# First tile of an attention tower: rows of ten 1000-row tables chosen by one-hot matmuls from whole tables, in place of gathers

## The chip, the core and the metric

The kernel runs on one core of a Trainium2 chip, in Bass, with the order of the work on each engine written out by hand. TensorE (PE) multiplies matrices from SBUF into PSUM, VectorE (DVE) and ScalarE (ACT) do elementwise work, GpSimd (POOL) issues the indirect DMAs here, and SyncE (SP) issues the plain ones. The metric is the device time of one execution in microseconds (us).

## What is computed

Thirty-three embedding tables of width 128 are looked up with 1024 x 33 ids; ten of the tables have 1000 rows, the others 1250, 12500 or 125000. All 528 pairs of the 33 rows of a sample are multiplied, sent through a layer, scored against a feature of the sample, weighted by a softmax and summed; a small network follows.

```
e = stack([tbl_f[ids[:, f]] for f in range(33)], axis=1)       # 1024 x 33 x 128
row, col = triu_indices(33, k=1)                               # 528 pairs
inner = e[:, row] * e[:, col]
fm = relu(einsum('bpd,ad->bpa', inner, attn_W) + attn_b)
attn = softmax(einsum('ba,bpa->bp', gnn_feature, fm), axis=1)
out = einsum('bp,bpd->bd', attn, inner) * 100
h = concatenate([gnn_feature, out, gnn_feature], axis=1)
h = relu(h @ W_top1 + b_top1); h = relu(h @ W_top2 + b_top2)
y = h @ W_top3
```

## The kernel before

The 1024 samples are taken in 8 tiles (t) of 128. A tile has 32 steps of 4 samples, so there are 256 steps (S), and each step works on 4 x 528 = 2112 columns.

**Rows into columns.** For each tile POOL gathers the 33 tables' rows into `x_rows`, one indirect DMA for each field (L259), in five groups of up to 8 fields: group c holds fields 8c to 8c+7, and group 4 the one field 32. When a group has landed (`rows_gathered`), PE transposes each field with the identity `ident` into one of three PSUM buffers `ring` (`transpose_x`, L574), and ACT copies the buffer into `xt` (`evacuate_xt`, L328). Groups 0 and 1 are copied once more behind field 32 (`repeat`, L318). `xt` has two buffers, one for each of two tiles. SP stores `x_rows` as a whole to DRAM (`store_rows`, L213) when all 33 gathers have landed; the gathers of the next tile wait for that store.

**A step.** DVE multiplies pairs of `xt` into `inner` (`product`, L405). Of the 5 chunks of a step (424 or 416 columns) some are multiplied by the attention weights directly in fp32 (L534, "native"; each shows as two records in the trace); for the rest ACT rounds `inner` to `inner_hi` (L298), DVE subtracts for `inner_lo` (L412), and PE makes three fp32r matmuls (L541 to L543). The first step has 4 native chunks, the second 3, later ones 1 or 2. ACT applies the relu into `fm` (L290), and PE reduces two steps at a time against `gnn_blocks` into `scores` (L564). Jobs of other tiles are laid between the steps: the transposes of tile t+1 at steps 18 to 26 of tile t, and `fields` (L592, fp32 matmuls of 128 x 128 with 128 columns) and the small network for tile t-1.

**The beginning.** SP issues the loads: ids, attention weights, features, bias, and then the six loads of the network (`mlp_weights_loaded`, 96 when all have landed), L215 to L224. PE transposes the features (L626). ACT waits for the network's loads before it rounds the attention weights (L349); DVE then makes `attn_wt_lo` (L467), adds two blocks of `w1_sb` (L470) and fills `gnn_blocks` (L419, L422). PE waits for these and for the network's loads before its first transpose of `x_rows`. DVE begins `product(0)` when all five groups are in `xt`, and PE begins `hidden(0)` after it.

## Time and profile before

| | us |
|---|---|
| runs before, median of 3 (lowest to highest) | 1273.31 (1273.05 to 1274.86) |
| the profiled execution, its own time | 1276.58 |
| its span in the profile | 1274.3 |
| first product on DVE starts | 52.18 |
| first matmul of a step on PE starts | 54.64 |

The span is the stretch that the profile covers; 2.3 us of the profiled execution's own time lie around it. An idle time in a row stands behind the instruction that ended it, with what released it. "Share of 16 engines" for a DMA queue is the time that its packets took over the stretch times 16.

### The profile page before, as it was taken

The page shows a single profiled execution, that of the slowest core. Times are in us where ns is not written, and L with a number is a line of the kernel's source. Part 1 is how long each engine was busy: PE and PEld are TensorE (multiplying, and loading weights), DVE is VectorE, ACT ScalarE, POOL GpSimd, SP SyncE. Part 2 cuts the span into 40 slices and gives each one's busy share as a digit, 9 for nine tenths or more (in the row PEclk, how much of TensorE's full clock was granted, in tenths as well). Part 3 has the DMA queues.
Part 4 walks back from the last instruction along what each step waited for, and adds up shares of the span by engine and source line. Part 5 has one row for each costly group of instructions (what it writes and reads, how often), then busy time and mean ns, then how long its engine had stood idle before and what let it go on. Part 6 is the DMA issues. An engine that isn't in the chain of part 4 may idle for free.

```text
span 1274.3 us, 21264 instructions
## 1 busy us (share of the span) xinstructions
PE 1207.8 (95%) x8752; PEld 902.5 (71%) x8752; DVE 1150.6 (90%) x643; ACT 1018.7 (80%) x1038; POOL 465.7 (37%) x271
## 2 busy tenths in 40 slices
PE   1499999999999999999999999999999999999998
PEld 1277777777777777777767777677776777777776
DVE  2399899998999989998999989999899998999974
ACT  1288998778887888878897788877888788887882
POOL 6586684018810387006840088102880000000000
PEclk9999999999999999999999999999999999999999
DMA  4213211311103111131102211031111300012100
GB/s 107 101 34 96 55 30 28 110 36 30 30 18 126 30 27 32 30 106 36 32 21 58 93 30 32 18 110 41 30 32 31 107 17 1 1 30 57 31 1 1
DMA packets 54287, 58.47 MB, mean 46 GB/s; under 512 B 10536, under 2 KB 48560, under 8 KB 53168
## 3 DMA queue, kind: packets, MB, share of 16 engines
q1 hardware_dynamic: 45728, 39.81, 10.5%
q0 software_dynamic: 8448, 17.32, 5.2%
q8 instruction: 69, 1.13, 0.4%
q14 instruction: 26, 0.21, 0.1%
q10 hardware_dynamic: 16, 0.00, 0.0%
HBM read 36.12 MB, written 17.31 MB: 42 GB/s over the span
## 4 chain that ended last, share of the span: by engine, by line
PE 78%; ACT 7%; issue 7%; DVE 6%; POOL 2%; DMA 0%; DVEq 0%; ACTq 0%; POOLq 0%
PE scores L564 18%; PE ring L534 16%; PE ring L541 12%; PE ring L542 11%; PE ring L543 11%; PE ring L592 3%; ACT fm L290 3%; DVE inner L405 3%; POOL x_rows L259 2%; PE ring L574 2%; ACT inner_hi L298 2%; DVE inner_lo L412 2%; PE ring L610 1%; DVE attn L447 1%; PE scores L621 1%
## 5 line engine op out<-in xcount | busy, mean ns | idle before, releaser
L290 ACT ACTIVATE fm<-ring,attn_b_sb 128x848 f32<-128x848 f32 (+1 forms) x640 | 596.9, 971 | 182.1 <-PE ring L534 175.7
L405 DVE TENSOR_TENSOR inner<-xt 128x2112 f32<-128x2112 f32 x256 | 602.7, 2354 | 67.5 <-ACT xt L328 37.4
L259 POOL DMA_INDIRECT x_rows<-in_tbl,ids_all x264 | 463.2, 1754 | 490.9 <-PE ring L574 401.2
L412 DVE TENSOR_TENSOR inner_lo<-inner,inner_hi 128x1688 fp32r<-128x1688 f32 (+4 forms) x256 | 467.0, 1824 | 25.8 <-ACT inner_hi L298 22.8
L541 PE MATMUL ring<-inner_hi,attn_wt_lo 128*128 128x424 f32 (+1 forms) x971 | 434.8, 448 | 4.2 <-ACT fm L290 3.5
L298 ACT CAST inner_hi<-inner 128x1688 fp32r<-128x1688 f32 (+4 forms) x256 | 392.3, 1532 | 5.1 <-DVE inner L405 5.0
L542 PE MATMUL ring<-inner_lo,attn_wt_hi 128*128 128x424 f32 (+1 forms) x971 | 344.3, 355 | 0.0
L543 PE MATMUL ring<-inner_hi,attn_wt_hi 128*128 128x424 f32 (+1 forms) x971 | 344.1, 354 | 0.0
L534 PE MATMUL ring<-inner,attn_wt 128*128 128x424 f32 (+1 forms) x618 | 276.6, 544 | 10.2 <-issue 6.5
L564 PE MATMUL scores<-fm,gnn_blocks 128*32 128x264 f32 x4096 | 254.6, 389 | 5.5 <-ACT exp_pairs L305 5.5
L541 PEld LDWEIGHTS ring<-inner_hi,attn_wt_lo 128*128 128x128 f32 x971 | 182.8, 188 | 71.8 <-issue 39.1
L542 PEld LDWEIGHTS ring<-inner_lo,attn_wt_hi 128*128 128x128 f32 x971 | 183.3, 189 | 43.5 <-issue 40.3
L564 PEld LDWEIGHTS scores<-fm,gnn_blocks 128*32 128x32 f32 x4096 | 119.9, 109 | 107.2 <-issue 13.9
L543 PEld LDWEIGHTS ring<-inner_hi,attn_wt_hi 128*128 128x128 f32 x971 | 182.5, 188 | 5.5
L534 PEld LDWEIGHTS ring<-inner,attn_wt 128*128 128x128 f32 x618 | 104.8, 190 | 85.5 <-issue 76.9
L274 POOL MEMSET inner<- 128x2048 f32 x1 | 1.8, 1811 | 279.0 <-PE ring L543 279.0
L574 PE MATMUL ring<-ident,x_rows 128*128 128x128 f32 x264 | 39.2, 292 | 34.1 <-DMA x_rows<-in_tbl,ids_all 31.3
L328 ACT COPY xt<-ring 128x1024 f32<-128x1024 f32 (+1 forms) x40 | 38.5, 966 | 31.6 <-PE ring L574 20.8
L574 PEld LDWEIGHTS ring<-ident,x_rows 128*128 128x128 f32 x264 | 33.0, 151 | 39.6 <-DMA x_rows<-in_tbl,ids_all 25.2
L592 PE MATMUL ring<-attn_t,x_fields 128*128 128x128 f32 x480 | 58.3, 275 | 1.1 <-issue 1.1
L592 PEld LDWEIGHTS ring<-attn_t,x_fields 128*128 128x128 f32 x480 | 58.0, 191 | 1.7 <-issue 1.5
L447 DVE TENSOR_TENSOR attn<-ring,xt 128x1024 f32<-128x1024 f32 x32 | 39.0, 1219 | 3.2 <-PE ring L592 2.9
(50 smaller groups left out, 250.3 us busy)
## 6 DMA issues: line engine op xcount, KB each, us to landing
x_dram<-x_rows SPq DMA_DIRECT2D x8, 2112.0 KB, 6.6
x_fields<-x_dram SPq DMA_DIRECT2D x120, 128.0 KB, 3.0
x_rows<-in_tbl,ids_all POOLq DMA_INDIRECT x264
attn_t<-attn_turned SPq DMA_DIRECT2D x112, 32.0 KB, 1.9
w_sb<-in_W_top SPq DMA_DIRECT2D x2, 512.0 KB
x_rows<-x_dram SPq DMA_DIRECT2D x8, 128.0 KB, 3.9
x_fields<-in_r_gnn_feature SPq DMA_DIRECT2D x1, 512.0 KB
h<-in_W_top SPq DMA_DIRECT2D x1, 256.0 KB
```

What stands on the lines that cost most here:

```text
L259: nc.gpsimd.indirect_dma_start(out=x_rows[:, f, :], out_offset=None, in_=tables[f], in_offset=bass.IndirectOffsetOnAxis(ap=ids_all[:, t, f ...
L290: nc.scalar.activation(dst, slot(("hidden", pair, j))[:, :, 0:n], ACT.Relu, bias=attn_b_sb[:, 0:1]).then_inc(s_fm, 1)
L298: nc.scalar.copy(inner_hi[:, S % HI_BUFS, 0:COLS - at], inner[:, S % INNER_BUFS, at:]).then_inc(s_hi, 1)
L405: nc.vector.tensor_tensor(dst, a, b, ALU.mult).then_inc(s_inner, 1)
L412: nc.vector.tensor_tensor(inner_lo[:, S % LO_BUFS, 0:COLS - at], inner[:, S % INNER_BUFS, at:], inner_hi[:, S % HI_BUFS, 0:COLS - at].bitc ...
L534: nc.tensor.matmul(dst, attn_wt[:], inner[:, S % INNER_BUFS, begin:end], start=True, stop=True)\
L541: nc.tensor.matmul(dst, attn_wt_lo[:], hi, start=True, stop=False)
L542: nc.tensor.matmul(dst, attn_wt_hi[:], lo, start=False, stop=False)
L543: nc.tensor.matmul(dst, attn_wt_hi[:], hi, start=False, stop=True).then_inc(s_hidden, 1)
L564: last = nc.tensor.matmul(scores[I * j:I * j + I, h, 0:HALF], block_of(s, j), fm[:, S % FM_BUFS, at:at + HALF], start=s == 0, stop=s == ST ...
L574: last = nc.tensor.transpose(to[:, n // 4, n % 4 * P:(n % 4 + 1) * P], x_rows[:, FU * c + n, :], ident[:])
L592: last = nc.tensor.matmul(bank[:, h, to:to + QS * I], x[:, n, :], own[:, :, n, :], start=True, stop=True)
```

## The change

For the first tile alone, the ten tables with 1000 rows (fields 2, 17, 21, 22, 23, 32, 26, 27, 29, 31, in this order) are loaded whole, 512,000 bytes each: 125 partitions with 8 rows of the table (4096 contiguous bytes) on each. The loads are ten DMAs that ACT issues as its first instructions. They land in `fm` and in `inner`, which are not used yet.

DVE puts the ids of the first tile on diagonals (`spread_ids`: memset, two casts and ten multiplications of 128 x 128, ahead of its other work), PE spreads them over all partitions with matmuls against ones (`put_ids_over`), and DVE compares them with row numbers from an `iota` on POOL (`choose`: one instruction of 128 x 1024 for each table, three buffers in the unused half of `xt`). PE then makes 8 accumulating fp32 matmuls for each table, with 125 rows of the table as weights and the one-hot columns moving. The result is the transposed field.

POOL gathers the other 23 fields first and these ten after them (their rows are still needed in `x_rows` for the store to DRAM, which now waits for them too). The groups of the first tile are taken in the order 0, 1, 2, 4, 3. PE gets 30 filler matmuls (ident by ident, 128 columns) before its wait for the last group's gathers and 10 after its transposes. `product(0)` is cut in two, one sample's 528 columns first, and PE's first chunk waits for the first piece alone.

```diff
-    units = [("x_t", 0, c) for c in range(XJ)]
+    units = [("x_t", 0, c) for c in XT_FIRST]
...
+            def gather_rows(t, f, signal):
...
                     for f in range(FU * c, FU * c + fields_in(c)):
-                        nc.gpsimd.indirect_dma_start(
-                            out=x_rows[:, f, :], out_offset=None, in_=tables[f],
-                            in_offset=bass.IndirectOffsetOnAxis(ap=ids_all[:, t, f:f + 1], axis=0),
-                        ).then_inc(s_gather[c], 16)
+                        if t > 0 or f not in ONE_HOT:
+                            gather_rows(t, f, s_gather[c])
+                if t == 0:
+                    for f in ONE_HOT:
+                        gather_rows(0, f, s_late)
...
+            for k, f in enumerate(ONE_HOT):
+                used = tables[f].shape[0] // PARTS
+                act.dma_start(small[k][0:used], tables[f].rearrange("(p c) d -> p c d", c=PARTS)).then_inc(s_tables[k], 16)
             act.wait_ge(s_small, 48)
             act.wait_ge(s_weights, 96)
...
+            def choose(k):
+                dve.wait_ge(s_ids_over, k // 4 + 1)
+                dve.wait_ge(s_row_of, 2)
+                if k >= CHOSEN:
+                    dve.wait_ge(*taken(k - CHOSEN))
...
+                nc.vector.tensor_tensor(chosen[k % CHOSEN], over, rows, ALU.is_equal).then_inc(s_chosen, 1)
...
+            def product_first():
+                x = xt[:, 0, 0:GROUPS, :]
+                dst = inner[:, 0].rearrange("d (g k f) -> d g k f", g=GROUPS, k=K)
+                for own, signal in ((slice(0, 1), s_first), (slice(1, GROUPS), s_inner)):
...
             gnn_block(0)
+            for k in range(len(ONE_HOT)):
+                choose(k)
             dve.wait_ge(s_xt_out, XJ)
             dve.wait_ge(s_repeat, K // FU)
-            product(0)
+            product_first()
             product(1)
...
+            def warm_up(n):
+                for _ in range(n):
+                    nc.tensor.matmul(scores[:, 0, 0:P], ident[:], ident[:], start=True, stop=True)
...
+                if t == 0:
+                    for f in own:
+                        if f in ONE_HOT:
+                            k = ONE_HOT.index(f)
+                            used = tables[f].shape[0] // PARTS
+                            pe.wait_ge(s_tables[k], 16)
+                            pe.wait_ge(s_chosen, k + 1)
+                            for p in range(PARTS):
+                                last = nc.tensor.matmul(home(f), small[k][0:used, p, :], chosen[k % CHOSEN][0:used, p, :],
+                                                        start=p == 0, stop=p == PARTS - 1, skip_group_check=True)
...
+                if t == 0 and c == XT_FIRST[-1]:
+                    warm_up(30)
+                pe.wait_ge(s_gather[c], rows_in(t, c))
...
             pe.wait_ge(s_setup, 6)
             pe.wait_ge(s_weights, 96)
-            for c in range(XJ):
+            for c in XT_FIRST[0:3]:
                 transpose_x(0, c)
-            pe.wait_ge(s_zero, 3)
+            put_ids_over(8, len(ONE_HOT))
+            for c in XT_FIRST[3:]:
+                transpose_x(0, c)
+            warm_up(10)
+            pe.wait_ge(s_zero, 4)
```

On PE, from the end of the setup to the first chunk of step 0, before (L574 are the transposes, L534 the first chunk):

```order
L574 MATMUL ring<-ident,x_rows 128x128 [waits rows_gathered0,mlp_weights_loaded,setup_copied]
L574 MATMUL ring<-ident,x_rows 128x128 x7
L574 MATMUL ring<-ident,x_rows 128x128 [waits rows_gathered1]
L574 MATMUL ring<-ident,x_rows 128x128 x7
L574 MATMUL ring<-ident,x_rows 128x128 [waits rows_gathered2]
L574 MATMUL ring<-ident,x_rows 128x128 x7
L574 MATMUL ring<-ident,x_rows 128x128 [waits x_t_evacuated,rows_gathered3]
L574 MATMUL ring<-ident,x_rows 128x128 x7
L574 MATMUL ring<-ident,x_rows 128x128 [waits x_t_evacuated,rows_gathered4]
L534 MATMUL ring<-inner,attn_wt 128x424 [waits x_t_evacuated,inner_ready,zeros_made]
```

The same place now, its beginning (L702 are the one-hot matmuls, with the table in `fm` as weights and the one-hot columns in `xt`; L711 the transposes; table 0 is field 2, table 1 field 17):

```order
L702 MATMUL ring<-xt,fm 128x128 [waits small_table_loaded0,one_hot_columns_made,mlp_weights_loaded,setup_copied]
L702 MATMUL ring<-xt,fm 128x128 x7
L711 MATMUL ring<-ident,x_rows 128x128 [waits rows_gathered0]
L711 MATMUL ring<-ident,x_rows 128x128 x6
L711 MATMUL ring<-ident,x_rows 128x128 [waits rows_gathered1]
L711 MATMUL ring<-ident,x_rows 128x128 x7
L702 MATMUL ring<-xt,fm 128x128 [waits one_hot_columns_made,small_table_loaded1]
```

and its end, from the last of the ten tables (L675 are the fillers, L638 the first chunk):

```order
L702 MATMUL ring<-xt,inner 128x128 [waits one_hot_columns_made,small_table_loaded9]
L702 MATMUL ring<-xt,inner 128x128 x7
L675 MATMUL scores<-ident 128x128 x30
L711 MATMUL ring<-ident,x_rows 128x128 [waits rows_gathered3]
L711 MATMUL ring<-ident,x_rows 128x128 x3
L675 MATMUL scores<-ident 128x128 x10
L638 MATMUL ring<-inner,attn_wt 128x424 [waits x_t_evacuated,first_products_ready,zeros_made]
```

Ten of the 33 transposes are replaced by 80 matmuls, which stand between the remaining 23, and 40 fillers are added. On ACT, before, the start of the program is the wait for the network's loads:

```order
L349 ACT_TABLE_LOAD [waits setup_copied,mlp_weights_loaded]
L349 CAST attn_wt_hi<-attn_wt 128x128 [waits small_inputs_loaded]
L328 COPY xt<-ring 128x128x8 [waits x_t_filled]
```

Now the ten loads of whole tables stand ahead of it:

```order
L405 DMA fm<-in_tbl 125x1024 x6
L405 DMA inner<-in_tbl 125x1024 x4
L409 ACT_TABLE_LOAD [waits setup_copied,mlp_weights_loaded]
L409 CAST attn_wt_hi<-attn_wt 128x128 [waits small_inputs_loaded]
L385 COPY xt<-ring 128x128x8 [waits x_t_filled]
```

Nothing is waited for ahead of them.

## Rows read from the trace of the kernel before

**Rows 1.** The page: busy time, TensorE by fortieth of the span, chain by engine.

```profile
PE 1207.8 (95%) x8752; PEld 902.5 (71%) x8752; DVE 1150.6 (90%) x643; ACT 1018.7 (80%) x1038; POOL 465.7 (37%) x271
...
PE   1499999999999999999999999999999999999998
...
PE 78%; ACT 7%; issue 7%; DVE 6%; POOL 2%; DMA 0%; DVEq 0%; ACTq 0%; POOLq 0%
```

**Rows 2.** The chain in order of time, 0 to 60 us: start, us, what.

```profile
4.50 1.14 POOL x_rows L259
5.94 0.94 POOL x_rows L259
...
22.18 0.94 POOL x_rows L259
...
43.39 2.43 DMA x_rows<-in_tbl,ids_all
46.00 2.18 PE ring L574 x9
48.18 6.46 issue
54.64 5.99 PE ring L534 x8
```

**Rows 3.** The timeline, 12 to 58 us: start, us, engine, line, instruction, idle before.

```profile
12.04 1.28 ACT L349 ACT_TABLE_LOAD   x1 [12.04 <-DMA b_sb<-in_b_top]
...
13.66 0.29 DVE L467 TENSOR_TENSOR attn_wt_lo<-attn_wt,attn_wt_hi 128x128 fp32r<-128x128 f32 x1 [3.56 <-ACT attn_wt_hi L349]
...
14.60 0.22 DVE L422 TENSOR_SCALAR gnn_blocks<-gnn_t 128x64 f32<-128x64 f32 x1
...
35.87 1.97 PE L574 MATMUL ring<-ident,x_rows 128*128 128x128 f32 x8 [7.90 <-DMA x_rows<-in_tbl,ids_all]
...
38.87 1.08 ACT L328 COPY xt<-ring 128x1024 f32<-128x1024 f32 x1 [8.62 <-PE ring L574]
...
50.79 1.35 ACT L328 COPY xt<-ring 128x1024 f32<-128x1024 f32 x2 [10.85 <-remote]
52.18 4.64 DVE L405 TENSOR_TENSOR inner<-xt 128x2112 f32<-128x2112 f32 x2 [37.36 <-ACT xt L328]
...
55.67 1.96 POOL L259 DMA_INDIRECT x_rows<-in_tbl,ids_all  x1 [0.31 <-issue]
```

**Rows 4.** DMA queues, 0 to 16 us: packets, MB, share of 16 engines.

```profile
q1 hardware_dynamic: 4384, 2.04, 47.2%
q0 software_dynamic: 256, 0.52, 12.7%
```

**Rows 5.** DMA queues and issues, 6 to 8.9 us (all queues that had packets).

```profile
DMA packets 675, 1.00 MB, mean 345 GB/s; under 512 B 36, under 2 KB 336, under 8 KB 675
## 3 DMA queue, kind: packets, MB, share of 16 engines
q1 hardware_dynamic: 675, 1.00, 97.1%
issues: line engine op xcount, KB each, median us to landing
x_rows<-in_tbl,ids_all POOLq DMA_INDIRECT x3
```

**Rows 6.** DMA queues, 47 to 54 us: one store of 128 rows.

```profile
q1 hardware_dynamic: 144, 2.16, 73.0%
```

**Rows 7.** DMA queues, 1262 to 1274.3 us: one store of a single row.

```profile
q10 hardware_dynamic: 2, 0.00, 0.0%
issues: line engine op xcount, KB each, median us to landing
out_y<-y_row ACTq DMA_DIRECT2D x1, 0.5 KB
```

**Rows 8.** The page's groups: busy us, mean ns of one.

```profile
L574 PE MATMUL ring<-ident,x_rows 128*128 128x128 f32 x264 | 39.2, 292 | 34.1 <-DMA x_rows<-in_tbl,ids_all 31.3
...
L592 PE MATMUL ring<-attn_t,x_fields 128*128 128x128 f32 x480 | 58.3, 275 | 1.1 <-issue 1.1
...
L447 DVE TENSOR_TENSOR attn<-ring,xt 128x1024 f32<-128x1024 f32 x32 | 39.0, 1219 | 3.2 <-PE ring L592 2.9
```

**Rows 9.** Groups on PE, 54.5 to 60.5 us.

```profile
L534 PE MATMUL ring<-inner,attn_wt 128*128 128x424 f32 x8 | 6.0, 930 | 6.5 <-issue 6.5
```

**Rows 10.** Groups on PE, 61 to 64.4 us.

```profile
L534 PE MATMUL ring<-inner,attn_wt 128*128 128x424 f32 (+1 forms) x6 | 2.3, 517 | 0.0
```

**Rows 11.** Stretches: us, then PE, PEld, DVE, ACT, POOL busy, clock, DMA.

```profile
62.00:114.00 52.00, 52.00 (x368) 37.80 (x367) 51.86 (x27) 45.26 (x44) 44.08 (x27) 1.00 0.14 35
```

**Rows 12.** The timeline of POOL, 114 to 136 us: the next tile's gathers.

```profile
117.38 1.97 POOL L259 DMA_INDIRECT x_rows<-in_tbl,ids_all  x1 [0.30 <-issue]
134.84 1.48 POOL L259 DMA_INDIRECT x_rows<-in_tbl,ids_all  x1 [15.49 <-PE ring L574]
```

More of the change, by code:

```diff
@@ L35, in afm_tower @@
     XJ = -(-F // FU)
+    PARTS = 8
+    ONE_HOT = [f for f in range(F) if tables[f].shape[0] <= PARTS * P and tables[f].shape[0] % PARTS == 0][:10]
+    XT_FIRST = (0, 1, 2, 4, 3)
+    ONE_HOT.sort(key=lambda f: (XT_FIRST.index(f // FU), f))
     I = F - 1
@@ L116, in afm_tower @@
         inv_sum = sb("inv_sum", [P, 1])
+        ids_first = sb("ids_first", [P, F])
+        row_of = sb("row_of", [P, PARTS], I32)
+        row_of_f = sb("row_of_f", [P, PARTS])
+        in_fm = FM_BUFS * COLS // (PARTS * D)
+        flat_fm, flat_inner = (b[:].rearrange("p r n -> p (r n)") for b in (fm, inner))
+        small = [flat_fm[:, k * PARTS * D:(k + 1) * PARTS * D] for k in range(in_fm)]
+        small += [flat_inner[:, k * PARTS * D:(k + 1) * PARTS * D] for k in range(len(ONE_HOT) - in_fm)]
+        small = [rows.rearrange("p (c d) -> p c d", d=D) for rows in small]
+        after = (len(ONE_HOT) - in_fm) * PARTS * D
+        ones = flat_inner[:, after:after + P]
+        diagonals = flat_inner[:, after + P:after + P + len(ONE_HOT) * P].rearrange("p (k b) -> p k b", b=P)
+        CHOSEN = 3
+        chosen = [xt[:, 1].rearrange("p b f -> p (b f)")[:, k * PARTS * P:(k + 1) * PARTS * P]
+                  .rearrange("p (c b) -> p c b", b=P) for k in range(CHOSEN)]
         gnn_rows = x_fields[:, 0, 0:T, :]
@@ L252, in _ @@
         def _(pool):
+            def gather_rows(t, f, signal):
+                nc.gpsimd.indirect_dma_start(
+                    out=x_rows[:, f, :], out_offset=None, in_=tables[f],
+                    in_offset=bass.IndirectOffsetOnAxis(ap=ids_all[:, t, f:f + 1], axis=0),
+                ).then_inc(signal, 16)
             def gather(t):
@@ L349, in _ @@
             nc.scalar.copy(attn_wt_hi[:], attn_wt[:]).then_inc(s_setup, 1)
-            for c in range(XJ):
+            for c in XT_FIRST:
                 evacuate_xt(0, c)
@@ L392, in _, with spread_ids @@
         def _(dve):
+            def spread_ids():
+                dve.wait_ge(s_ids, 16)
+                nc.vector.memset(ones, 1.0).then_inc(s_zero, 1)
+                nc.vector.tensor_copy(ids_first[:], ids_all[:, 0, :]).then_inc(s_diagonal, 1)
+                dve.wait_ge(s_row_of, 1)
+                nc.vector.tensor_copy(row_of_f[:], row_of[:]).then_inc(s_row_of, 1)
+                dve.wait_ge(s_diagonal, 1)
+                dve.wait_ge(s_const, 2)
+                for k, f in enumerate(ONE_HOT):
+                    nc.vector.tensor_scalar(diagonals[:, k, :], ident[:], ids_first[:, f:f + 1], None, ALU.mult)\
+                        .then_inc(s_diagonal, 1)
+            def choose(k):
[3 more added lines that the diff above has]
+                    dve.wait_ge(*taken(k - CHOSEN))
+                over = ids_over(k)
+                part, sample = over.ap
+                over = bass.AP(tensor=over.tensor, offset=over.offset, ap=[part, [0, PARTS], sample])
+                rows = row_of_f[:]
+                part, row = rows.ap
+                rows = bass.AP(tensor=rows.tensor, offset=rows.offset, ap=[part, row, [0, P]])
+                nc.vector.tensor_tensor(chosen[k % CHOSEN], over, rows, ALU.is_equal).then_inc(s_chosen, 1)
[3 more added lines that the diff above has]
+                for own, signal in ((slice(0, 1), s_first), (slice(1, GROUPS), s_inner)):
+                    a = x[:, own, 0:F]
+                    part, sample, field = a.ap
+                    a = bass.AP(tensor=a.tensor, offset=a.offset, ap=[part, sample, [0, K], field])
+                    b = x[:, own, 1:1 + F]
+                    b = bass.AP(tensor=b.tensor, offset=b.offset, ap=[part, sample, [1, K], field])
+                    nc.vector.tensor_tensor(dst[:, own], a, b, ALU.mult).then_inc(signal, 1)
             def product(S):
@@ L525, in hidden @@
             def hidden(S):
-                pe.wait_ge(s_inner, S + 1)
+                if S == 0:
+                    pe.wait_ge(s_first, 1)
+                else:
+                    pe.wait_ge(s_inner, S + 1)
                 for c in range(CHUNKS):
+                    if S == 0 and c == 1:
+                        pe.wait_ge(s_inner, 1)
                     begin, end = EDGES[S % 2][c:c + 2]
```

57 lines of the change are left out of this document (47 added, 10 removed).

## The prediction, made before the changed kernel was run

> **What bounds the kernel now.** I read the page first: PE is busy for 95% of the span and holds 78% of the chain, and of the forty slices the first two alone are thin [rows 1]. From 62 us on PE has no idle time at all in 52 us [rows 11]. So the steps are PE's, the change leaves them as they are, and what it can move is when they begin. I therefore read the beginning, the chain in order of time [rows 2] and then the timeline [rows 3]. POOL issues 33 gathers, the first at 4.50, the second at 5.94, the fifteenth at 22.18: 1.25 us each (0.94 and a gap of 0.3). The last but one starts at 43.39, and PE goes on at 46.00, 1.67 us after its issue ended. Nine transposes, two copies on ACT and the first product follow; DVE starts it at 52.18 and PE its first chunk at 54.64. Between the transposes' end (48.18) and the copies (50.79) lie 2.6 us that the trace puts down to "remote", a cause it does not name. The mark that I follow is the **start of the first product, 52.18 us**; all that comes after moves with it.
>
> **What is removed.** Ten of the 33 gathers leave the path: 10 x 1.25 = 12.5 us. The 23rd gather would land at 33.1 + 1.67 = 34.8 instead of 47.2. If gathers were all, the first product would come some 12 to 15 us earlier. So everything depends on what takes their place.
>
> **The loads of ten tables.** Each has 512,000 bytes. An engine's rate: the store moved 2.16 MB with 73.0% of 7 us on 16 engines [rows 6], 26.4 GB/s for each engine; the network's loads moved 1.00 MB with 97.1% of 2.9 us [rows 5], 22.2 GB/s. On how many engines does such a load run? The store of 128 rows left 144 packets, its 128 rows and 16 more, one from each engine [rows 6]. The store of a single row left 2, one row and one more, so it ran on one engine [rows 7]. A DMA's shape thus sets its engines. 16 divides 128; it does not divide the 125 partitions of a table, whose only divisors up to 16 are 5 and 1. I take equal shares, so **5 engines** with 25 rows each: 102,400 bytes at 26.4 GB/s are 3.88 us for a table, **38.8 us for ten** (46.1 at the lower rate). On 16 engines it would be 1.21 us each and 12.1 us in all (14.4); I keep that end. No row shows a DMA of 125 partitions.
>
> The Trainium skill, page "DMA: Bandwidth & Descriptors", section "Why a DMA increments its semaphore by 16 and not by 1", speaks against this change: the number of engines is the largest up to 16 that divides both sides' slowest dimension, on the low-numbered engines, and 100 partitions give 10. By it 125 give 5. The packets of rows 6 and 7 agree with it at 16 and at 1.
>
> **Who waits behind them.** ACT issues the ten as its first instructions, beside SP's ten. Both go to the same DMA engines. What a queue does to another shows between 6 and 8.9 us: the first gather had been issued by 5.64 and the second by 6.88, three more were being issued, and yet only q1, SP's queue, moved packets, 97.1% of the time [rows 2, 5]; a gather else lands 1.67 us after its issue. So work waits for what was queued ahead of it, and I let that hold here for the first five engines: ids, network's loads and gathers need all 16 to land, and these five have 38.8 us of table rows to get through.
>
> The same page, section "Queues, rings and completion order", has each engine take turns between queues packet by packet. Rows 5 do not agree, since a gather would have had its turn at 6.9. By turns the forecast would stay: SP's queue has 4384 packets, 274 for each engine [rows 4], against 250 table rows on each of the five, so SP's last loads would still come near the end.
>
> SP's loads keep an engine busy for 47.2% of 16 us, 7.6 us [rows 4]. Behind each other this makes 7.6 + 38.8 = 46.4 us; counted from before's landing it is 12.04 + 38.8 = 50.8, if none of the 4.4 us in which the engines were idle gets filled. I take 49.5 us for the network's loads. The 23 gathers have 16 x 12.7% / 8 = 0.25 us each on an engine, so they all land by about 55, before PE needs them.
>
> **PE and DVE after that.** From the landing to the last `gnn_blocks` instruction it takes 14.82 - 12.04 = 2.78 us [rows 3]. The first `choose` is 128 x 1024 with one operand in PSUM as L447 is: 1.22 us [rows 8]. PE's first one-hot matmul: 49.5 + 4.0 = **53.5**. One fp32 matmul of 128 columns is two records; at full speed a record costs 58.3 / 480 = 0.121 us [rows 8], so a table of 8 costs 1.94. The beginning runs at half speed: eight records of 424 columns take 6.0 us at 54.64, six take 2.3 us after 61 [rows 9, 10], 0.75 against 0.38 each, that is 1.2 and 2.4 GHz, though the clock column says 1.00. PE worked for 6.4 us before that rise, and I let it do so here. In PE's order:
> - table 0, half speed: 3.9, to 57.4; 15 transposes at 1.97 / 8 [rows 3]: 3.7, to 61.1. The clock rises here.
> - four tables of group 2: 7.8; four transposes at (39.2 - 33 x 0.246) / 231 = 0.135 [rows 8]: 0.5; the ids of two tables, 256 columns: 0.5; field 32: 1.9. To 71.8.
> - four tables of group 3: 7.8, to 79.6; **30 fillers, 60 records: 7.3**, to 86.9. No wait is left for them to fill, because the gathers have long landed, so they are paid in full. Four transposes: 0.5, to 87.4.
> - ACT's copy: 1.1 [rows 3], to **88.5**.
>
> So the first product starts 36.3 us later. The other `choose` lie beside PE's work (1.22 against 1.94 for a table, three buffers). The 10 last fillers (2.4 us) lie beside ACT's copy and the first piece (1.1 + 0.6).
>
> **What the clock and the two pieces give back.** PE would begin its chunks at full speed. At most that gives half of 6.4 us, 3.2. But DVE needs product, rest, product: its second `product` ends 4.64 us after the first starts whatever PE does [rows 3], and from 62 to 114 us it is busy for 51.86 of 52 us [rows 11]. I take 1.0.
>
> **At nothing:** the diagonals, casts and iota (DVE idles until 13.66, when the rounded weights are there [rows 3], and longer now). The ten late gathers and the later store: the next tile's gathers end 15.49 us before POOL's next wait is over [rows 12]; ten gathers beside DVE at 1.96 instead of 0.94 [rows 3] would take 10 of that, and here PE is later by more. Without this cover the store's delay would add to the time one for one.
>
> **Sum.** 36.3 - 1.0 = +35.3 us. Against the profiled execution's own 1276.58 that is 1311.9; it stands 3.3 above the median, so against 1273.31 it is **1308.6**, rounded to 1308.
>
> **Rivals.**
> - **A, the tables take five engines but hold up only themselves.** For it: two queues may share better than SP's and POOL's did. The last table lands at 49.5, then 1.9 + 7.3 + 0.5 + 1.1: first product at 60.3, or 65 where PE between tables is at half speed. +7 to +12 after the 1.0: 1280 to 1285.
> - **B, all 16 engines.** Network's loads at 12.04 + 12.1 = 24.1, PE from 28.1, and the same 35.0 us of work as above: 63.1, +9.9, 1283. Where they hold up nothing, PE has to wait for the fifteenth gather (23.1 + 1.7 = 24.8), then 2.0 for its group, and 7.8 + 0.5 + 0.5 + 1.9 + 7.8 + 7.3 + 0.5 + 1.1 = 27.4: 54.2, +1.0, 1274. Against it: 16 does not divide 125.
> - **C, faster: the shorter row of gathers shows.** One mechanism: the loads stay out of the way as in B's second case and the full clock gives back all of its 3.2 us, with the 2.6 us before ACT's last copies gone as well, which the 54.2 already has. Then 54.2 - 52.18 - 3.2 = -1.2, and with group 1 transposed at full speed and a shorter pass of the tables, about -3: 1270. It decides from where the last one-hot matmul ends by 41.8 us, since 7.3 + 0.5 + 1.1 follow and 50.7 is wanted. PE's 17.6 us for nine tables after 26.8 speak against it.
> - **D, the change doesn't hold the clock:** PE falls or stays at half speed among waits for tables or DVE. Up to 6.4 us of it cost 3.2 more, and the lower rate of an engine 7.3 more: 1312 to 1319.
>
> **How the numbers follow.** The forecast has 0.51, D 0.06, A 0.17, B 0.13 (0.05 of it near 1274), C 0.13. The range reaches from B's lower case and part of C to the lower engine rate: 1272 to 1318. It is wide because the cases lie far apart; the likeliest alone has 1303 to 1316. About 0.2% (2.5 us) is what a measurement of this kernel can tell from no change: faster 0.13, same 0.07, slower 0.80.
>
> **What would show it.** In the new profile: the loads of the tables landing some 3.9 us apart until about 48 (1.2 apart: B); ACT's table load starting at about 49 instead of 12.04 (about 12 to 20: A); few or no gathers' packets before the tables are through; fillers right behind the last one-hot matmul, with the gathers long landed; the first product at about 88. I am wrong if the one-hot matmuls begin before 30 us.

## The result, and the profile after

| | us |
|---|---|
| changed kernel, median of 5 runs (lowest to highest) | 1316.62 (1316.08 to 1317.23) |
| kernel before, its 5 runs together | 1273.31 (1272.76 to 1274.86) |
| ratio, 95% interval | 1.034 (1.0329 to 1.0351) |
| profiled execution after, its own time; its span | 1316.44; 1314.7 |

The change makes the kernel 43.3 us slower. The prediction said 1308 with a range of 1272 to 1318: the direction and most of the size hold, the way in which the queues share the engines does not, and 8.6 us are missing in the sum. On the page of the new profile the first line is busy time, then TensorE by fortieth, then the chain, as in [rows 1]:

```profile
PE 1233.3 (94%) x8988; PEld 927.6 (71%) x8988; DVE 1165.0 (89%) x667; ACT 1018.3 (77%) x1038; POOL 456.2 (35%) x272
...
PE   0299999999999999999999999999999999999998
...
PE 76%; DVE 7%; ACT 7%; issue 5%; DMA 2%; SPq 2%; DVEq 0%; ACTq 0%
```

From the third slice on TensorE is as full as before. Only the beginning is different, and the chain in order of time shows it (start, us, what; compare [rows 2]):

```profile
2.40 11.09 SPq L267
...
29.08 28.99 DMA b_sb<-in_b_top
...
58.13 1.28 ACT L409
...
62.18 3.75 PE ring L702 x16
65.93 2.29 PE ring L711 x15
68.22 7.15 PE ring L702 x64
...
76.24 8.93 PE ring L702 x80
85.17 6.70 PE scores L675 x60
91.87 0.45 PE ring L711 x4
92.35 1.09 ACT xt L385
93.46 2.43 DVE inner L487 x2
```

The last of the network's loads is 1 KB of biases. It lands at 58.1 us, where it was 12.04 before [rows 3]. Behind it stand the setup, the one-hot matmuls, and 6.7 us of fillers that fill no wait. The first product starts at 93.46.

SP itself was held up: to issue a load of 512 bytes (L267) kept its queue for 11.09 us. GpSimd's first gather, before at 4.50 [rows 2], waits for the ids:

```profile
15.90 1.14 POOL L303 DMA_INDIRECT x_rows<-in_tbl,ids_all  x1 [14.32 <-DMA ids_all<-in_ids]
```

What the DMA engines do meanwhile is the reading that matters most. The queues from 8 to 14 us (packets, MB, share of 16 engines; q10 is ACT's queue with the tables, q1 is SP's with the ids):

```profile
DMA packets 370, 0.76 MB, mean 127 GB/s; under 512 B 190, under 2 KB 190, under 8 KB 370
...
q10 hardware_dynamic: 185, 0.74, 29.9%
q1 hardware_dynamic: 185, 0.02, 2.7%
```

Equal counts: for each 4096-byte packet of a table one of the ids' small ones went through. And 29.9% of sixteen engines are 4.8 engines: the tables ran on five. A slice of 0.2 us, 9.0 to 9.2, shows both directly, five packets of the one and five of the other:

```profile
q10 hardware_dynamic: 5, 0.02, 24.9%
q1 hardware_dynamic: 5, 0.00, 2.2%
```

The busy time from 8 to 14 us, 0.299 x 6 x 16 = 28.7 us, over the 181 packets that 0.74 MB make (4 more are tiny end packets) is 0.159 us each. From 48 to 56 us, shortly before the tables' end, all three kinds are there (q0 is GpSimd's queue), and the counts of q10 and q1 are equal again:

```profile
q10 hardware_dynamic: 212, 0.85, 26.6%
q0 software_dynamic: 210, 0.41, 17.2%
q1 hardware_dynamic: 212, 0.00, 1.6%
```

In some stretches between, SP's queue has many more packets (423 to 45 from 28 to 30 us). The other eleven engines hold no tables, so nothing takes turns with SP's packets from that queue there.

TensorE in the new order: stretches, columns as in [rows 11], the last but two of which is the clock:

```profile
62.00:68.00 6.00, 5.82 (x31) 5.85 (x32) 3.52 (x4) 0.61 (x1) 0.38 (x1) 0.57 0.42 180
68.00:92.00 24.00, 24.00 (x216) 23.95 (x214) 7.35 (x6) 5.19 (x6) 18.21 (x20) 1.00 0.21 53
```

After 22 us of idling TensorE runs at half speed (1.2 GHz) for the first 4.9 us of its work: the granted clock is 0.50 up to 67.0 us and 0.86 in the half microsecond behind it. From then on it is 1.00 (2.4 GHz).

### The profile page after: what moved, and what is told of

Same layout as the page of the kernel before. It is cut to its first block, busy times and chain, and to the rows that moved or that the text cites. A ratio compares the mean times of both kernels' runs of the same rounds, so it can differ in the third digit from the quotient of the medians.

```text
span 1314.7 us, 21800 instructions
## 1 busy us (share of the span) xinstructions
PE 1233.3 (94%) x8988; PEld 927.6 (71%) x8988; DVE 1165.0 (89%) x667; ACT 1018.3 (77%) x1038; POOL 456.2 (35%) x272
## 4 chain that ended last, share of the span: by engine, by line
PE 76%; DVE 7%; ACT 7%; issue 5%; DMA 2%; SPq 2%; DVEq 0%; ACTq 0%
PE scores L668 18%; PE ring L638 15%; PE ring L645 12%; PE ring L646 11%; PE ring L647 11%; DVE inner L501 3%; ACT fm L347 3%; PE ring L729 3%; PE ring L711 2%; DMA b_sb<-in_b_top 2%; DVE inner_lo L508 2%; ACT inner_hi L355 2%; PE ring L702 2%; PE ring L747 1%; DVE attn L543 1%
## 5 line engine op out<-in xcount | busy, mean ns | idle before, releaser
L303 POOL DMA_INDIRECT x_rows<-in_tbl,ids_all x264 | 453.6, 1718 | 543.4 <-PE ring L711 451.3
L638 PE MATMUL ring<-inner,attn_wt 128*128 128x424 f32 (+1 forms) x618 | 273.9, 538 | 4.4 <-ACT fm L347 3.7
L638 PEld LDWEIGHTS ring<-inner,attn_wt 128*128 128x128 f32 x618 | 103.6, 188 | 78.5 <-issue 68.1
L729 PEld LDWEIGHTS ring<-attn_t,x_fields 128*128 128x128 f32 x480 | 57.9, 191 | 1.7 <-issue 1.5
L409 ACT ACT_TABLE_LOAD x1 | 1.3, 1283 | 58.1 <-DMA b_sb<-in_b_top 58.1
L550 DVE TENSOR_REDUCE pooled<-attn 128x32 f32<-128x1024 f32 x32 | 38.8, 1213 | 0.1
```

Of the source, the lines that this page charges most:

```text
L303: nc.gpsimd.indirect_dma_start(out=x_rows[:, f, :], out_offset=None, in_=tables[f], in_offset=bass.IndirectOffsetOnAxis(ap=ids_all[:, t, f ...
L638: nc.tensor.matmul(dst, attn_wt[:], inner[:, S % INNER_BUFS, begin:end], start=True, stop=True)\
L729: last = nc.tensor.matmul(bank[:, h, to:to + QS * I], x[:, n, :], own[:, :, n, :], start=True, stop=True)
```

## The experiments

The theory after this reading has three parts. (a) The ten loads run on five engines because of their 125 partitions. (b) What costs most is not that they are slow but that SP's loads, thousands of tiny packets, take turns with them packet by packet. (c) The 30 fillers are paid in full. Rivals: the tables' bytes as such hold things up, whatever their shape and queue; the fillers hold the clock and pay for themselves.

### The tables on sixteen engines

```diff
-                act.dma_start(small[k][0:used], tables[f].rearrange("(p c) d -> p c d", c=PARTS)).then_inc(s_tables[k], 16)
+                src = tables[f].rearrange("(p c) d -> p c d", c=PARTS)
+                act.dma_start(small[k][0:112], src[0:112]).then_inc(s_tables[k], 16)
+                act.dma_start(small[k][112:used], src[112:used]).then_inc(s_tables[k], 16)
...
-                            pe.wait_ge(s_tables[k], 16)
+                            pe.wait_ge(s_tables[k], 32)
```

> The changed kernel with each table loaded by two DMAs, 112 partitions and 13 partitions, in place of one of 125; same bytes, same consumers. Theory (shape sets the engines): 112 runs on 16 engines and 13 on 13, so the ten tables need about 12 us of each engine instead of 40 us of five. ids, taking turns with the tables' packets, still land late, at about 13 (after: 15.7); the network's loads land at about 24 instead of 58; the first product starts at 60 to 62 instead of 93.5, so about 1285 us. Rival (the 5 MB themselves cost this, on whatever engines): no change, 1316.

Measured: 1295.74 us (1294.9 to 1297.27), ratio 1.0177 (1.016 to 1.0194). A change of shape alone gives 21 us. ACT's table load starts at 37.68 instead of 58.13, the first product at 72.33. Part (a) holds, but not its size: about 1285 was expected. The queues from 20 to 28 us:

```profile
DMA packets 857, 2.11 MB, mean 263 GB/s; under 512 B 192, under 2 KB 199, under 8 KB 857
...
q10 hardware_dynamic: 319, 1.04, 50.4%
q1 hardware_dynamic: 320, 0.60, 30.2%
q0 software_dynamic: 218, 0.46, 23.0%
```

Again as many packets of q10 as of q1, so the turns of part (b) show a second time. But a 4096-byte packet now takes 0.504 x 8 x 16 / 254 = 0.25 us (1.04 MB are 254 of them), against 0.16 on five engines, and all together move 263 GB/s where I had reckoned with over 400 [rows 6].

### The tables behind the network's loads

The split undone; the ten loads of 125 partitions stand at the end of SP's queue, behind the network's, instead of on ACT's.

```diff
             sp.dma_start(b2_sb[:], b2.rearrange("(m p) -> p m", p=P), allow_slow_non_contiguous=True).then_inc(s_weights, 16)
+            for k, f in enumerate(ONE_HOT):
+                used = tables[f].shape[0] // PARTS
+                sp.dma_start(small[k][0:used], tables[f].rearrange("(p c) d -> p c d", c=PARTS)).then_inc(s_tables[k], 16)
```

> The changed kernel with the ten loads of 125 partitions moved from ACT's queue to the end of SP's own, behind the network's loads. Theory (two queues take turns packet by packet, one queue works in order): ids land at about 3.6 and the network's loads at about 12, as before the change; the tables still take 40 us of five engines plus the gathers' turns and end at about 58, PE follows them one by one, and the first product starts at 68 to 72: 1291 to 1296 us. Rival (gathers wait for everything queued ahead of them, as the prediction had it): the gathers land after 52, PE has all its work after that, first product at about 80: 1303.

Measured: 1291.53 us (1290.95 to 1293.01), ratio 1.0144 (1.0128 to 1.0161), as expected. Not a byte, a packet or an engine less than in the changed kernel, and 25 us are gone. The network's loads land by 13.31, the one-hot matmuls start at 17.42. Now the tables bound the beginning, as the chain says:

```profile
34.62 22.97 DMA inner<-in_tbl
57.59 0.04 issue
57.63 2.10 PE ring L702 x16
59.73 6.70 PE scores L675 x60
```

The run also decides about the gathers. From 14 to 22 us 208 of their packets go through beside 217 of the tables, whose loads SP had been issuing since 7.08, and group 1 is transposed at 26.71. So gathers do not wait for the tables queued ahead of them, and the rival's 1303 is out. And it separates what the first run could not: a queue's order costs more here (25 us) than the five engines (21 us).

### Without the 30 fillers

```diff
                 if t == 0 and c == XT_FIRST[-1]:
-                    warm_up(30)
+                    pass
```

> The changed kernel without the 30 fillers (the 10 later ones stay). Theory (no wait is left for them): the first product starts 6.7 us earlier, 86.8, and the time falls by 6 to 7 us to 1310. Rival (they keep TensorE's clock up for what follows): less than that is gained, 3 us or none, and the last transposes and first chunks run at half speed.

Measured: 1310.26 us (1310.07 to 1310.45), ratio 1.0288 (1.0271 to 1.0305): 6.4 us less than with them. The loads land 0.8 later in the profiled run (58.93), the first product starts at 87.63. The clock does not fall, and part (c) holds:

```profile
68.00:86.00 18.00, 18.00 (x162) 17.95 (x161) 7.44 (x7) 5.81 (x6) 13.25 (x15) 1.00 0.19 49
```

### The kernel before once more

> The kernel before, unchanged, for a second profile. The first profile had ACT wait 2.6 us longer than PE's transposes for its last two copies of the first tile and its execution lay 3.3 us above the median. If these belong together, a profile near the median shows ACT's copy right behind the transposes, at about 48.2, and the first product at about 49.6. If the wait is part of every execution, the copy starts at 50.8 again and the execution may still be near 1273.3.

Measured: 1273.63 us (10 runs), ratio 1.0002 (0.9993 to 1.0012), profiled execution 1272.89. In its timeline ACT's last copies are released by PE and not "remote", and the product starts 3.0 us earlier than in [rows 3]:

```profile
47.80 1.35 ACT L328 COPY xt<-ring 128x1024 f32<-128x1024 f32 x2 [8.82 <-PE ring L574]
49.19 4.63 DVE L405 TENSOR_TENSOR inner<-xt 128x2112 f32<-128x2112 f32 x2 [34.18 <-ACT xt L328]
```

So the wait of rows 3 belongs to that one execution. The shift of the first product is 93.46 - 49.19 = 44.3 us, the times differ by 43.3, and 1.0 is given back.

### What the change could have been

The tables from SP's queue behind the network's loads, each in 112 + 13 partitions, no 30 fillers, and TensorE takes group 2's one-hot matmuls ahead of group 1's gathers:

```diff
+                sp.dma_start(small[k][0:112], src[0:112]).then_inc(s_tables[k], 16)
+                sp.dma_start(small[k][112:used], src[112:used]).then_inc(s_tables[k], 16)
...
-            for c in XT_FIRST[0:3]:
-                transpose_x(0, c)
+            transpose_x(0, 0)
+            transpose_x(0, 2, rest=False)
+            transpose_x(0, 1)
+            transpose_x(0, 2, one_hot=False)
```

> The changed kernel with four edits: the tables' loads on SP's queue behind the network's, each split into 112 and 13 partitions; no 30 fillers; and PE makes the one-hot matmuls of group 2 before it waits for group 1's gathers. Theory: network's loads at 12 to 13, one-hot matmuls from 17.4; tables land some 2.5 us apart from 13 on, the last at 35 to 38; PE fills its waits for gathers and ends its last transposes at 40 to 43; first product at 41 to 45 against 49.2 in the kernel before: 1265 to 1269 us, faster than before. Rival (the tables' loads at 16 engines slow the gathers so much that the 23rd lands after 45, as each gather took 7.5 us to land in the split run): first product at 48 or later, 1272 or more.

Measured: 1271.42 us (1270.52 to 1273.03, 11 runs), ratio 0.9988 (0.9979 to 0.9997): 45 us better than the changed kernel and about level with before, short of the 1265 to 1269 expected. The first product starts at 47.95. The gathers take turns with the tables and land 5.0 us after their issue, and TensorE waits for those of group 2:

```profile
34.83 1.12 PE L716 MATMUL ring<-ident,x_rows 128*128 128x128 f32 x4 [4.25 <-DMA x_rows<-in_tbl,ids_all]
```

The same with one load of 125 partitions for each table:

> As the reworked kernel, but each table is loaded by one DMA of 125 partitions again. If the five engines set the pace, the last table lands at 57.6 as in the same-queue run, and the first product starts at 57.6 + 2.1 + 0.5 + 1.1 = 61.3: 1284 to 1286 us. If order and fillers were what mattered and not the engines, it lies within 3 us of the reworked kernel.

Measured: 1285.03 us (1284.63 to 1285.19), ratio 1.0093 (1.0078 to 1.0109), as expected. The last table lands at 57.9, and its matmuls, group 3's four transposes and ACT's copy put the first product at 61.64. The split alone is worth 13.6 us here.

### The fillers and the two pieces alone

Before, with 20 fillers in the wait for group 3, 10 after the transposes, and the product in two pieces; no tables.

```diff
-            product(0)
+            product_first()
...
+                if t == 0 and c == 3:
+                    warm_up(20)
```

> The kernel before with two parts of the change alone: fillers (20 in the wait for group 3's gathers, 10 after the last transposes) and the product in two pieces; no one-hot rows. Theory: the first chunks run at full speed, and since DVE sets the pace there, 1.0 us is gained: 1272.3. Rival one: all 3.2 us of the half-speed stretch come back: 1270. Rival two: the fillers still run when group 3's gathers land at 45.8 and cost up to 1 us: no gain.

Measured: 1272.7 us (11 runs), ratio 0.9995 (0.9986 to 1.0004): no difference that can be measured. In a real wait the fillers do what they are for, and nine transposes take 1.52 us where they took 2.18 [rows 2]:

```profile
38.05 6.38 PE L588 MATMUL scores<-ident 128*128 128x128 f32 x40
...
46.30 1.52 PE L597 MATMUL ring<-ident,x_rows 128*128 128x128 f32 x9 [1.88 <-DMA x_rows<-in_tbl,ids_all]
```

But the chunks then wait for DVE, whose row is as long as before. The value of a fast clock at the beginning is the 0.7 us ahead of the product, and little of that arrives.

### Why sixteen engines were slow

There are three runs. The first is the first experiment's kernel with 64 + 48 + 13 partitions:

> As the first split run, but with 64, 48 and 13 partitions in place of 112 and 13, still from ACT. In the split run a 4096-byte packet took 240 to 280 ns with all engines busy, against 160 on five engines, and the network's loads landed at 37.7 instead of the 24 expected. If the 7 partitions per engine of the 112 (engines meeting on the same part of SBUF) cause this, 4 and 3 per engine bring the packets nearer to 160 ns and the landing to 30 or less. If the sum of all 16 engines is what is limited, both stay: 240 to 280 ns and 36 to 39, about 1295 us.

Measured: 1300.84 us (two runs), ratio 1.0217 (1.0198 to 1.0236). The network's loads land at 43.47, and all queues together move 228 GB/s from 10 to 40 us. Nothing is gained by a finer split; it is 5 us slower. Then the kernel of the next section with the first tile's gathers held back until the tables are in:

> The kernel of the run before this one (TensorE's waits filled) with one more wait: GpSimd starts the first tile's gathers when all ten tables are in. So the tables' 4096-byte packets are alone on the sixteen DMA engines. In the runs with 112 and 13 partitions these packets took 240 to 300 ns beside the gathers' (160 ns on five engines). If the gathers' packets (turns on the same engine, random rows in DRAM) slowed them, they take about 160 ns here, the engines move about 400 GB/s, and ten tables (5.1 MB) are through 12 to 13 us after the network's loads, at 26 to 27. If sixteen engines reading these tables reach no more than some 260 GB/s in all, they take 240 ns and more here too, and the last table is in at 32 or later. The time itself is longer by the gathers' delay and says nothing.

and the same with 128 partitions in one load, from the first 1024 rows of ten larger tables, so it leaves out the rows that the ten one-hot fields need:

> The kernel e10b_gathers_held with one DMA of 128 partitions for each table in place of the two of 112 and 13: it reads the first 1024 rows of ten larger tables, so the ten one-hot fields are wrong here; the work of all engines is the same, and the gathers are again held until the loads are in. In e10b the 4096-byte packets had the sixteen engines to themselves and still took 0.26 us each (519 of them in 8 us, 266 GB/s), against 0.16 us on five engines. The gathers were not the cause. If it is the shape (7 partitions an engine and a 13th part on one or few engines behind it), 8 equal partitions an engine take about 0.16 us here, some 400 GB/s, and ten loads of 524,288 bytes (5.24 MB) are through some 13 us after the network's loads, at 26 to 27. If sixteen engines that read whole rows of tables into 4096 contiguous bytes of a partition get no more than some 260 to 270 GB/s whatever the split, the packets take 0.25 us or more, and the first gather is issued at 31.5 or later (31.39 in e10b).

From 14 to 22 us the tables' queue has the engines to itself in both. With 112 + 13 partitions:

```profile
DMA packets 628, 2.09 MB, mean 261 GB/s; under 512 B 118, under 2 KB 118, under 8 KB 628
## 3 DMA queue, kind: packets, MB, share of 16 engines
q1 hardware_dynamic: 628, 2.09, 103.6%
```

With 128:

```profile
DMA packets 907, 3.31 MB, mean 413 GB/s; under 512 B 100, under 2 KB 100, under 8 KB 907
...
q1 hardware_dynamic: 907, 3.31, 102.7%
```

A 4096-byte packet takes 1.036 x 8 x 16 / 510 = 0.26 us in the one and 1.027 x 8 x 16 / 807 = 0.16 us in the other; the first gather is issued at 31.39 and at 26.40. (Their times, 1299.88 and 1325.0, contain the gathers' delay and say nothing here.) So neither the gathers nor sixteen engines as such make the packets slow. What remains is that the last run changed two things together, the split and the tables that are read; which of them counts was not tried. 64 + 48 + 13 being no faster speaks against "7 partitions an engine" alone. It does not rule out that several engines meet on the same part of SBUF in each of these splits: no run varied which partitions are written at the same time.

### A version that beats both

The reworked kernel with group 4 second and group 3's one-hot matmuls ahead of group 2's transposes (the edit is shown against the changed kernel):

```diff
-    XT_FIRST = (0, 1, 2, 4, 3)
+    XT_FIRST = (0, 4, 1, 2, 3)
...
-            for c in XT_FIRST[0:3]:
-                transpose_x(0, c)
+            transpose_x(0, 0)
+            transpose_x(0, 4)
+            transpose_x(0, 2, rest=False)
             put_ids_over(8, len(ONE_HOT))
-            for c in XT_FIRST[3:]:
-                transpose_x(0, c)
+            transpose_x(0, 1)
+            transpose_x(0, 3, rest=False)
+            transpose_x(0, 2, one_hot=False)
+            transpose_x(0, 3, one_hot=False)
```

> The reworked kernel again (tables from SP's queue behind the network's loads, each in two loads of 112 and 13 partitions, no 30 fillers), with TensorE's row of work in another order: group 4's one-hots (one field, no gather) right behind group 0, then group 2's, then group 1's transposes, then group 3's one-hots before group 2's transposes are waited for. In the reworked kernel TensorE waited 4.25 us at group 2's gathers (34.83) and then ran 2.61 + 7.31 us of one-hots behind them, with the first product at 47.95. Theory (what is left at the front is TensorE's order alone, since the tables are through by 35): group 3's 64 one-hot matmuls (7.3 us) fill the wait from 30.5 on, group 3's four gathers land at about 38 to 39, the last transposes end at about 40, ACT's copy takes 1.1, and the first product begins at 41 to 42.5, 5.5 to 7 us earlier; the time is 1264.5 to 1266. Rival (the last table or the gathers of group 3 come later than the reworked kernel's trace lets one see, since they take turns with the tables' 4096-byte packets): first product at 45 or later, 1268.5 or more.

Measured: 1274.33 us (1267.36 to 1278.48, 12 runs), ratio 1.0005 (0.9993 to 1.0018). The first product starts at 43.03, nearly as expected and 4.9 us earlier than in the reworked kernel, and yet the time is 2.9 us longer than there, where 1264.5 to 1266 was expected. Only one of the twelve executions came near, with 1267.36. In the profiled one the gain is given back 100 us later. Rows of GpSimd and TensorE, start and us first:

```profile
55.19 40.41 POOL L308 DMA_INDIRECT x_rows<-in_tbl,ids_all  x1 [8.91 <-DMA x_dram<-x_rows]
...
147.22 1.94 PE L716 MATMUL ring<-ident,x_rows 128*128 128x128 f32 x8 [3.79 <-DMA x_rows<-in_tbl,ids_all]
```

One gather of the next tile took 40.41 us, where its neighbours take 1 to 2 (3.13 at most in the kernels so far, but for the one with the gathers held). The cover of 15.49 us [rows 12] was gone, and TensorE waited again for 1.52 us at 160.84. What ended it? DVE's rows then:

```profile
90.61 2.35 DVE L503 TENSOR_TENSOR inner<-xt 128x2112 f32<-128x2112 f32 x1
92.88 1.90 DVE L510 TENSOR_TENSOR inner_lo<-inner,inner_hi 128x1688 fp32r<-128x1688 f32 x1
94.77 2.36 DVE L503 TENSOR_TENSOR inner<-xt 128x2112 f32<-128x2112 f32 x1
```

Since the gather began each instruction had started 0.07 to 0.09 us before the end of the last (92.88 against 92.96). The one at 94.77 is the first without such an overlap but for 0.01, and the gather ended at 95.60, 0.83 us behind it. In the run with the gathers held the same happened (30.42 us, ended at 117.53; the instruction with an overlap of 0.02 began at 116.69). So I gave DVE one pause, hidden because TensorE needs that product 14 us later:

```diff
+                        if t == 1 and f == 0:
+                            nc.gpsimd.iota(row_of[:], pattern=[[1, PARTS]], base=0, channel_multiplier=PARTS).then_inc(s_row_of, 1)
...
+                    if S == 5:
+                        dve.wait_ge(s_row_of, 3)
                     product(S + 3)
```

> The kernel e9b_three_waits_filled with one pause in VectorE's row: ahead of the product of step 8 (70.98 in that run) VectorE waits until GpSimd has issued the first gather of tile 1 and run one small iota. In that run the first product began at 43.03 (47.95 in the reworked kernel), but the first gather of tile 1 took 40.41 us (55.19 to 95.60; 0.94 to 3.0 in the other kernels), TensorE waited 3.79 us at 147.22 and the gain of 5 us was gone; one of its twelve runs took 1267.36. The same happened in e10b_gathers_held (30.42 us, to 117.53). In both VectorE ran back to back, each instruction starting 0.07 to 0.09 us before the last one's end, and the gather ended 0.83 and 0.84 us behind the first product whose overlap was only 0.01 to 0.02. Theory (VectorE's unbroken row of two-input instructions keeps the gather waiting, and it gets in at the first gap): the gather ends by about 71, the pause is under 2 us and hidden (TensorE needs the product of step 8 at about 85), the gathers run to about 137, no wait at 147, and the time is 1266 to 1268. Rival (the hold is not VectorE's doing): the gather again takes some 40 us, VectorE stands still until it ends, and the time is 1285 or more. Second rival (the 5 us are given back elsewhere): gathers in time, and yet 1271 or more.

Measured: **1266.11 us** (1265.81 to 1268.05), ratio 0.9945 (0.9932 to 0.9959). It beats both kernels, 7 us better than before and 50 better than the changed one. The rows say why:

```profile
55.80 16.76 POOL L308 DMA_INDIRECT x_rows<-in_tbl,ids_all  x1 [8.85 <-DMA x_dram<-x_rows]
...
69.83 1.91 DVE L512 TENSOR_TENSOR inner_lo<-inner,inner_hi 128x1688 fp32r<-128x1688 f32 x1
72.57 0.15 POOL L322 IOTA row_of<- 128x8 int32 x1
72.75 2.36 DVE L505 TENSOR_TENSOR inner<-xt 128x2112 f32<-128x2112 f32 x1 [1.02 <-POOL row_of L322]
```

The gather was caught again, DVE stopped at 71.74 (69.83 + 1.91), and the gather ended at 72.56, 0.82 us later. The pause cost DVE 1.02 us and TensorE nothing. That DVE's unbroken row is what holds the gather is now shown, since stopping it set the gather free. Two more gathers were held in this kernel, and no gap freed them:

```profile
208.01 15.79 POOL L308 DMA_INDIRECT x_rows<-in_tbl,ids_all  x1 [0.30 <-issue]
222.85 1.27 DVE L547 TENSOR_TENSOR attn<-ring,xt 128x1024 f32<-128x1024 f32 x1
227.51 10.41 POOL L308 DMA_INDIRECT x_rows<-in_tbl,ids_all  x1 [0.30 <-issue]
236.97 1.27 DVE L547 TENSOR_TENSOR attn<-ring,xt 128x1024 f32<-128x1024 f32 x1
```

They ended at 223.80 and 237.92, each 0.95 us after an L547 instruction began. Its one input lies in PSUM (`ring`), and it is the first since the gather's start that does not have two inputs in SBUF, though DVE's row goes on there with overlaps of 0.13 and 0.14. So what holds a gather is the row of instructions with two SBUF inputs, and one of another kind in the row seems to free it as a pause does; no run was made to test this. TensorE never waited for a gather in this kernel.

The Trainium skill, page "SBUF — State Buffer", section "Who interferes with whom", says that a VectorE instruction with two SBUF inputs contends with a GpSimd instruction that reads SBUF, as an exclusive lock held for the whole instruction. The traces agree in kind (both DVE lines of the row have two such inputs, L547 has one). The same section reports a probe in which `tensor_tensor` did not stall a DMA, and gives an inferred reason. Here rows of it held a gather for 10 to 40 us, and the measurement decides. The traces also go further in size: the gather got no turn in nineteen instructions one after the other, which that section does not state. Why other gathers pass in 1 to 3 us beside the same row stays open.

## Why the prediction was right, and where it was off

- **The loads run on five engines**: right. The tables' queue keeps 29.9% of sixteen busy, 4.8 engines, and the split over sixteen takes 21 us off (13.6 in the reworked kernel). 0.159 us for 4096 bytes is 25.8 GB/s an engine from 8 to 14 us, where the prediction took 26.4; over the whole beginning the rate was lower (see the landing below).
- **The network's loads wait for the tables**: right as an outcome, wrong as a mechanism. The prediction let work wait for what was queued ahead of it, by [rows 5], and set the rule of turns aside because a gather had no turn there. This is the step that failed. The runs show turns: 185 to 185 packets, 319 to 320. The prediction's own sign, few or no gathers' packets before the tables are through, did not appear: GpSimd's queue moved 1006 of its 1056 packets from 15 to 57 us. With the tables behind the loads in the same queue 25 us went away, and the gathers still got through. Both mechanisms gave about the same landing here, as the prediction itself says, so the time could not tell them apart; the packet counts could. What rows 5 show of a first gather beside a busy SP queue is then something else. No run looked at that.
- **Landing at 49.5**: off by 8.6 us (58.1), the largest mis-sized term. Two things lengthen it. With turns the gathers' packets come in ahead of SP's last ones: up to 58.1 us their queue has 13.1% of the sixteen engines' time, 0.131 x 58.1 = 7.6 us on each. The prediction had put just these 23 to 33 times 0.25 us behind the landing, where they would have cost nothing. And the tables' packets took longer than the 38.8 us of the sum: their queue has 23.9% up to 58.1 us, 222 us in all or 44.4 on each of five engines. That is 23.1 GB/s an engine, between the prediction's two rates (26.4 and 22.2). SP's queue has 16.1%, 9.4 us on an engine against 7.6. The three make 61.4 us of packets in 58.1, so packets' times overlap, and how the 8.6 us divide between the turns and the lower rate is not shown.
- **From the landing to the product, 39.0 us predicted, 35.3 measured** (58.13 to 93.46): the setup and the first `choose` took 4.05 (4.0 predicted); TensorE's part and ACT's copy took 31.3 instead of 35.0. The clock rose after about 4.9 us of work and not after the first 7.6, so in the chain the fifteen transposes took 2.29 (3.7), 1.4 of the 3.7 us. Most of the rest lies in the terms at full speed, each right within a tenth: 7.15 for four tables (7.8), 8.93 for one and four more (9.7), 6.70 for the fillers (7.3).
- **The fillers are paid in full**: right, 6.4 us by the run without them.
- **1.0 given back by clock and pieces**: right in size (44.3 less 43.3; the spans of the two profiled executions, 1314.7 and 1270.9, leave 0.5). That clock and pieces gave it is not shown. On the kernel before, fillers and pieces together were worth 0.4 us, with an interval that takes in nothing.
- **At nothing**: right. The next tile's gathers did not come too late in the changed kernel. The cover does exist, as the run at 1274.33 shows, where it was used up.
- **Size against the median**: the prediction's start of 52.18 held 3.0 us of a wait that only the profiled execution had. The sum took the 3.3 us between 1276.58 and the median off at its end and yet counted the shift from 52.18, so this wait was subtracted without being a gain. Of the missing 8.6 us 3.0 come from there, 5.0 from the first product at 93.46 instead of 88.5 (landing 8.6 later, 3.7 less work), and 0.6 from rounding 1308.6 down. That the time lies near the forecast is in part luck: two errors of the sum had opposite signs.
- **Rivals.** A (the tables hold up only themselves) is nearest to the run with the tables behind SP's loads: 1291.53, first product at 68.03, above its 1280 to 1285, since the last table landed at 57.6 and not at 49.5. The 1285.03 of the reworked kernel with 125 partitions lies where A had it only because the fillers, which A's sum holds, are gone there. B's 1283 and 1274 did not come about: on sixteen engines the kernel took 1295.74, as the split's rate was 263 GB/s. C, the faster one, needed the last one-hot matmul by 41.8 with the fillers behind it; in the last version it ends at 41.15 without fillers, and the time is 1266. D's 1312 to 1319 holds the measured 1316.62, while the likeliest case alone had 1303 to 1316. Its clock did not fall (1.00 from 68 us on), but its lower engine rate was there in part.

## What to carry to other kernels

Before loading something large early, ask what small loads will share its engines. A queue of many tiny packets that takes turns with 4096-byte ones runs at the large packets' pace: 1 KB of biases came 46 us late. Put the large load behind the small ones in the same queue, and give it a shape that spreads over all engines. And look a hundred microseconds further for each gain at the beginning: here it was lost at GpSimd, and a pause of 1 us in the engine with time to spare brought it back.

## What the runs showed of the hardware

- Of two issuing queues each gets as many packets as the other on shared engines, whatever their size (185 to 185 and 212 to 212; 319 to 320; 5 to 5 in a slice of 0.2 us). The Trainium skill, page "DMA: Bandwidth & Descriptors", section "Queues, rings and completion order", states such turns; the traces agree.
- 125 partitions run on five engines, 4.4 us of each for 512,000 bytes in the mean of ten loads (44.4 us); 112 + 13 on sixteen at 261 GB/s, 128 at 413 GB/s. The difference between the last two is not explained.
- With much queued, issuing itself stalls: SP's L267 took 11.09 us for a load of 512 bytes, 0.58 in the kernel before.
- A gather's issue on GpSimd can be held for 40.41 us by an unbroken row of VectorE instructions with two SBUF inputs. It ended 0.82 to 0.84 us behind the first pause or the first overlap of 0.02 us or less in the row (three gathers), or 0.95 us behind the start of an instruction with an input in PSUM (two).
